# Part stores in one transfer a quarter, and three products of the first stage in other places

## The reference

```python
xn = _layernorm(x, axis=-1)
# _L0_attn_ref, on xn
x2 = _layer_norm(xn, ln1_g, ln1_b)
q, k, v = x2 @ wq + bq, x2 @ wk + bk, x2 @ wv + bv          # 16 heads of 16 channels
p = jnp.einsum('blhd,dm->blhm', x, proj_mat) / math.sqrt(D_HEAD)   # x: q or k, 128 maps
feature = jnp.concatenate([jnp.cos(p), jnp.sin(p)], axis=-1) / math.sqrt(D_KMAP)
kv = jnp.einsum('blhm,blhd->bhmd', kp, v)
attn = jnp.einsum('blhm,bhmd->blhd', qp, kv)
s = ...   # attn @ wo + bo, residual, layer norm, w1, relu, w2, residual
# _L0_ffn_ref, on xn
xr = mu_r * x + (1.0 - mu_r) * x_prev
xk = mu_k * x + (1.0 - mu_k) * x_prev
r = jax.nn.sigmoid(jnp.einsum('btc,dc->btd', xr, W_r))      # "receptance"
k_act = jnp.square(jax.nn.relu(jnp.einsum('btc,dc->btd', xk, W_k)))
out = r * jnp.einsum('btc,dc->btd', k_act, W_v)             # "value" product
x = x + s * _silu(out)
```

## Time and profile before

| what | us |
| --- | --- |
| median of 3 runs (range) | 2329.96 (2327.01 to 2332.29) |
| the profiled execution, device time | 2326.66 |
| its span, first to last instruction | 2324.9 |
| features of batch 0, first to last L456 | 57.33 to 157.07 |
| features of batch 1, first to last L456 | 280.57 to 379.06 |
| first L456 of batches 2 and 3 | 502.49, 722.41 |

### The profile page before, as it was taken

How to read it: one execution, slowest core, us unless ns; L and a number is a source line. 1 busy time by engine, 2 the same in 40 slices (tenths; PEclk the granted TensorE clock), 3 DMA queues, 4 the chain that set the end, 5 groups by cost and what they waited for, 6 DMA issues and landing times. The chain is left out here.

```text
span 2324.9 us, 24556 instructions
## 1 busy us (share of the span) xinstructions
PE 1963.6 (84%) x7316; PEld 1006.5 (43%) x7332; DVE 1717.9 (74%) x2363; ACT 1217.3 (52%) x1646; POOL 1223.2 (53%) x651
## 2 busy tenths in 40 slices
PE   5699879978996898889989998899886678997995
PEld 3336534643463355333324332433242235665663
DVE  4984598369827933699999999999989993223887
ACT  3873486268526732566654665466544433443542
POOL 2601351053107110288788899989977672212664
PEclk9899989989999999999999999999989999999997
DMA  6510640073007312788889898988899982223442
GB/s 163 137 37 0 163 108 20 0 200 83 9 19 182 73 37 64 107 300 290 284 278 313 283 284 291 317 282 294 288 307 373 329 302 76 93 89 100 136 136 79
DMA packets 182690, 402.57 MB, mean 173 GB/s; under 512 B 49454, under 2 KB 78384, under 8 KB 181410
## 3 DMA queue, kind: packets, MB, share of 16 engines
q1 hardware_dynamic: 170530, 371.10, 52.1%
q0 software_dynamic: 12032, 29.90, 4.5%
HBM read 356.30 MB, written 45.51 MB: 173 GB/s over the span
## 5 line engine op out<-in xcount | busy, mean ns | idle before, releaser
L1191 POOL TENSOR_TENSOR late<-late,rows 128x1024 f32<-128x1024 f32 x256 | 602.9, 2364 | 146.8 <-DVE late L1667 138.0
L1840 PE MATMUL m_Q<-late,ident_m 128*128 128x512 f32 x1024 | 528.9, 649 | 150.5 <-POOL late L1191 113.1
L1667 DVE TENSOR_TENSOR_SCAN late<-m_Q,late 128x1024 f32<-128x1024 f32 x256 | 586.2, 2290 | 44.8 <-ACT m_Q L1377 16.4
L1377 ACT ACTIVATE m_Q<-late,acol 128x1024 f32<-128x1024 f32 x256 | 286.1, 1118 | 361.5 <-DVE late L1667 359.3
L1840 PEld LDWEIGHTS m_Q<-late,ident_m 128*128 128x128 f32 x1024 | 195.4, 203 | 450.9 <-POOL late L1191 261.0
L1660 DVE TENSOR_TENSOR late<-m_Q,rows 128x1024 f32<-128x1024 f32 x256 | 306.9, 1199 | 12.8 <-DMA rows<-bc_s 12.7
L290 POOL TENSOR_TENSOR qkh<-early,qkh 128x1024 bf16<-128x1024 f32 x16 | 33.8, 2126 | 286.8 <-ACT qkh L561 286.8
L1559 ACT ACTIVATE late<-m_Q,e_b1c 128x128 f32<-128x128 f32 x312 | 88.9, 368 | 181.1 <-PE m_Q L1909 180.8
L456 DVE SCALAR_TENSOR_TENSOR early<-early,work 128x1024 f32<-128x1024 f32 x128 | 155.8, 1217 | 25.4 <-ACT early L598 23.0
L606 ACT ACTIVATE early<-early 128x1024 f32<-128x1024 f32 x128 | 134.8, 1053 | 49.1 <-DVE early L461 47.8
L1900 PE MATMUL m_Q<-early,late 128*128 x312 | 149.0, 600 | 2.7 <-issue 2.0
(11 more groups left out here) (233 smaller groups left out, 3393.5 us busy)
## 6 DMA issues: line engine op xcount, KB each, us to landing
rows<-bc_s SPq DMA_DIRECT2D x512, 512.0 KB, 5.8
rows<-st_s SPq DMA_DIRECT2D x64, 384.0 KB, 5.7
st_s<-qkh SPq DMA_DIRECT2D x128, 96.0 KB, 2.4
r_s<-late SPq DMA_DIRECT2D x39, 256.0 KB, 2.0
rows<-st_s SPq DMA_DIRECT2D x32, 256.0 KB, 6.5
xin<-in_x SPq DMA_DIRECT2D x4, 1024.0 KB, 10.2
xres<-in_x SPq DMA_DIRECT2D x4, 1024.0 KB, 7.3
mx_s<-s SPq DMA_DIRECT2D x4, 1024.0 KB, 4.5
```

The lines of the kernel that those rows point to most:

```text
L1191: nc.gpsimd.tensor_tensor(pr[:, n % NH, :], h[:, n % NH, :], cb[:, n % NCB, :], ALU.mult).then_inc(pr_ok, 1)
L1377: A(dA[:, :], dt[:, (b * KI + m) % 2, :], ACT.Exp, scale=acol[:, m, i % NS:i % NS + 1]).then_inc(dA_ok, 1)
L1667: v_.tensor_tensor_scan(h[:, n % NH, :], dA[:, :], dB[:, n % 2, :], 0.0, ALU.mult, ALU.add).then_inc(h_ok, 1)
L1840: ins = mm(half(Y, c), ident[:, :], half(pr[:, n % NH, :], c), start=False, stop=(n % NS == NS - 1), skip_group_check=True)
```

## The change

In `phase_a`, part stores: a quarter is stored by one transfer of 128 partitions instead of eight of 16, to a DRAM tensor with channels ahead of parts; a unit is loaded by four transfers (48, 48, 16, 16 partitions) instead of three (48, 48, 32). SP's order becomes store 0, unit 0, store 1, unit 1, store 2, and store 3 only inside the features, ahead of unit 2.

Products: `q1` leaves the stretch before the features and is made in steps 0 and 1; `xn`, `gl` and `gate` of the previous batch are made in steps 2, 4, 7 and 12. `kk` moves from steps 20 and 26 to 9 and 14, `vv` from behind `wo` to steps 20 and 25, and `r` from steps 13 and 17 to behind `wo`, with its Tanh reading PSUM. On POOL `low(3)` stands ahead of the mixtures, and xk is mixed before xr. In the scan, at nine steps a batch, ACT takes a link of a sigmoid before a PSUM evacuation instead of after it.

```diff
-AMID = {13: ("r", 0), 17: ("r", 1), 20: ("kk", 0), 26: ("kk", 1)}
-TAKEN = {15: ("r", 0), 19: ("r", 1), 22: ("kk", 0), 28: ("kk", 1)}
+AMID = {0: ("q", 1), 9: ("kk", 0), 14: ("kk", 1), 20: ("vv", 0), 25: ("vv", 1)}
+RELU = {11: 0, 16: 1}
+VALUE = {21: 0, 26: 1}
+PREVIOUS = {2: ("xn", 0), 4: ("xn", 1), 7: ("gl",), 12: ("gate",)}
...
 def parts_out(b, q):
     sp.wait_ge(lo_ok, b * 4 + q + 1)
-    for hd in range(8):
-        sp.dma_start(g["st_s"][q, hd].rearrange("s c t -> c s t"), parts[DH * hd:DH * hd + DH, q % 2, :, :]).then_inc(part_out[q % 2], 16)
+    sp.dma_start(g["st_s"][q].rearrange("h c s t -> (h c) s t"), parts[:, q % 2, :, :]).then_inc(part_out[q % 2], 16)
...
+def first_units(b):
+    parts_out(b, 0)
+    unit_in(b, 0)
+    parts_out(b, 1)
+    unit_in(b, 1)
+    parts_out(b, 2)
...
@@ SP @@
 def batch(b, last):
+    parts_out(b, 3)
+    unit_in(b, 2)
+    if b:
+        turned_out(b - 1)
+    unit_in(b, 3)
...
@@ POOL @@
 for b in range(B):
     pool.wait_ge(tr_ok, b * 6 + 4)
     if b:
-        pool.wait_ge(lg_ok, b)
+        pool.wait_ge(out_ok, b * 2)
+    low(b, 3)
+    pool.wait_ge(lo_ok, b * 4 + 4)
+    mixture(b, 1)
     mixture(b, 0)
-    mixture(b, 1)
...
@@ ACT, behind the two Sin of step s @@
+if s == 1:
+    high(b, 3)
+elif s == 3:
+    middle(b, 3)
+elif s in VALUE:
+    i = VALUE[s]
+    wait_full(ac, b, "vv", i)
+    A(kr[:, i, :], slot(b, "vv", i)[:, :], ACT.Identity).then_inc(vv_ok, 1)
...
@@ ACT, scan, step 15 of block1 @@
+sigmoid(b + 1, "conv", 1, 1)
 evacuate(b + 1, "z", 1, 0)
-sigmoid(b + 1, "conv", 1, 1)
```

More of the change, by code:

```diff
@@ L60, in sequence @@
     for b in range(B):
[L61 to L65, removed]
+        seq += body(b)
+        if b + 1 < B:
+            seq += [(b + 1, j) for j in PRE]
+        else:
+            seq += [(b, j) for j in [("mx", m) for m in range(2 * KD)] + [("xn", 0), ("xn", 1), ("gl",), ("gate",)]]
     return seq
@@ L213, in _ @@
                     load(t[:, :, :], matrix(n), a_in)
[L214 to L215 removed]
+                for s in range(3):
+                    for p in (0, 3 * DH):
+                        load(prj[p + s:p + 3 * DH:3, :], g["proj"], p_in)
+                for s in range(2):
+                    load(prj[(6 + s) * DH:(7 + s) * DH, :], g["proj"], p_in)
                 with nc.allow_non_contiguous_dma(reason="vectors by channel, once"):
@@ L509, in batch @@
                         remainder(b + 1, 2)
-                        remainder(b + 1, 3)
-                    wait_full(dv, b, "gate")
-                    v_.tensor_copy(g["lg"][:, bass.ds(b * TB, TB), :],
-                                   slot(b, "gate")[:, 0:TB * E].rearrange("p (t e) -> p t e", t=TB)).then_inc(lg_ok, 1)
+                    if last:
+                        gate_logits(b)
                     assert n[0] == (DVE_LINKS if last else DVE_LINKS + 2 * LN_LINKS)
@@ L524, in _ @@
                 prepare()
-                for q in range(4):
+                for q in range(3):
                     remainder(0, q)
@@ L542, in _, with high, middle @@
                 ac.wait_ge(prep, 4)
+                def high(b, q):
+                    name, m = SPLIT[q]
+                    wait_full(ac, b, name, m)
+                    if q >= 2 or b:
+                        ac.wait_ge(part_out[q % 2], (b * 2 + q // 2) * 16)
+                    A(parts[:, q % 2, 0, :], slot(b, name, m)[:, :], ACT.Identity, bias=cols[:, "qk".index(name), m:m + 1]).then_inc(hi_ok, 1)
+                def middle(b, q):
+                    ac.wait_ge(r1_ok, b * 4 + q + 1)
+                    A(parts[:, q % 2, 1, :], rest(q), ACT.Identity).then_inc(mid_ok, 1)
                 def before_features(b):
@@ L633, in batch @@
                             A(xi4[:, m, 3:3 + L], slot(b, "mx", m)[:, :], ACT.Identity).then_inc(mx_ok, 1)
-                        normed(b)
+                        for c in range(NC_):
+                            normed(b, c)
                         logits(b)
```

215 lines of the change are left out of this document (104 added, 111 removed).

## The result

| | before | after |
|---|---|---|
| median (range), 4 runs each | 2328.49 (2323.80 to 2332.29) | 2358.99 (2357.27 to 2360.53) |
| ratio, 95% interval | 1 | 1.0130 (1.0111 to 1.0149) |
| span of the profiled execution | 2324.9 | 2358.2 |

The changed kernel is 30.5 us slower. The prediction had the sign, 12 us of the amount, and a range that ended at 2354.

The account below looks back on a forecast made before the run. No engine was taken to bound the whole kernel; DVE sets the features' pace. 3 x 2.9 + 8.0 - 4.7 = +12.0 on 2326.66 gave 2338.7, as a median 2342, stated as 2341; range 2318 to 2354.

Parts of the forecast that it names:

- The start: Start of the features: first rounding subtraction 12.2 us earlier in batch 1, 5.6 earlier in batch 0.
- Steps 0 to 3: First feature steps: part of the gain given back, step 3 14.4 us behind the first subtraction where it was 9.1.
- Step 9: PE waits for the first mixture, late behind low(3), before kk; step 9 starts 5.5 us later in batch 1.
- Step 9 to the end (a small gain): Features from step 9 to the last subtraction: -2.6 us together, from copies, masks and evacuations.
- Batch 0: Features of the first batch: last subtraction 8 us later, with step 9 11 us later, less 2.6.
- The scan: Scan stage: a sigmoid link fills ACT's wait before an evacuation, DVE regains 4.7 us over three batch changes.
- More waits: Rival, slower still: late squares or kk and vv slots cost each batch 3 us more, 2353; chance 0.1.
- The mixture is in time: Rival, faster: the first mixture doesn't hold PE at step 9, 2293, or 2318 with half the wait; chance 0.25.
- It cancels: Rival, same: start, stall and scan come out within 4.7 us of nothing; chance 0.2.

Follow-up runs that it names:

- before_store: The kernel before with only the storage part of the change (one store a quarter, four loads a unit, their orders on SP and ACT): 2354.99 us, ratio 0.9993.
- before_scan: The kernel before with only the eight scan exchanges, sigmoid link ahead of the PSUM evacuation: 2355.67 us against 2358.36, ratio 0.9993.
- unit2_first: The changed kernel with SP loading unit 2 ahead of storing quarter 3: 2357.33 us, ratio 1.0121 to the kernel before.
- kk_later: The changed kernel with kk at steps 12 and 15, its relu at 14 and 17, vv at 22 and 26: 2375.74 us, ratio 1.0208.
- mix_first: The changed kernel with POOL's first mixture ahead of low(3) and unit 2 loaded ahead of store 3: 2348.07 us against 2358.50, ratio 0.9951.
- gate_read_13: The changed kernel with DVE's copy of the previous batch's gate logits in step 13, not 14: 2348.75 us, ratio 1.0086.
- mix_first_gate: mix_first with the edit of gate_read_13 added: ratio 0.9934 to the kernel before.
- q1_before_act_order: q1_before with gate logits read in step 13, gate product read behind step 6, and ACT's order ahead of the features changed: 2321.57 us, ratio 0.9859.
- q1_before: The changed kernel with the second query half and quarter 3 back ahead of the features: 2344.35 us, ratio 0.9946.

## Why the prediction was right in sign and short in size

Against the prediction's steps, in us. The whole was +12.0 predicted and +33.3 between the two spans.

- **The start.** Predicted -12.2; measured -12.6, -12.5 and -11.1 in batches 1 to 3: right. Batch 0: -5.6 predicted, -4.2 measured; there I gave it to the order of `middle` and to the second quarter's stores, and before_store, which has both, starts at 57.57, against 57.33 before and 59.62 in before_scan. So these two alone do not give it; what does stays open. This start also scatters: after, unit2_first and kk_later are alike up to there and start at 53.17, 53.59 and 50.30.
- **Steps 0 to 3.** Predicted 14.4 to step 3 and 20.0 to the end of `middle(3)`; measured 14.9 and 20.4. Right.
- **Step 9.** Predicted 43.6 behind the first subtraction, with the mixture at +40.0 and the half product at half clock, 3.7; measured 44.2 to 44.5, +40.0, 3.68. Right, and unit2_first shows that of unit 2 and the mixture the latter binds. What I did not see is the third wait at the same place (the gate product's slot, 2.49 us in mix_first), which costs nothing while the mixture is last. Before, step 9 stood at 25.2 and not 25.9 in batches 2 and 3, which makes the stall 0.7 longer there.
- **Step 9 to the end (a small gain).** This is the step that failed: its term of -2.6 counted copies, masks and evacuations and put PE's waits for PSUM slots at nothing. Predicted -2.6 a batch; measured +0.6, +2.1, +0.7, +1.0. That is 4.4 + 10.4 = 14.8 of the 21.3 us that the sum is short. gate_read_13 names about half of it: `kk(1)` in step 14 takes the slot of the gate logits, which DVE reads in step 14, and PE runs at half clock behind the wait. Without it these steps take 7.2 us less over the three batches that have a previous batch, and mix_first_gate takes 7.75 off mix_first there. Batch 0, which has no such wait, was 1.1 us shorter too, and 2.3 shorter in unit2_first (70.12), so part of its miss is scatter. With the wait gone, batches 0 to 3 are at -0.5, 0.0, -1.3 and -2.2 of before, and at -1.1 to -1.6 in batches 0 to 3 of mix_first_gate: the gain is there, but smaller than the -2.6, and why is not shown beyond what follows. The "about 1 us less by my count" for POOL beside DVE's masks did not come: the collision of the earlier trace rows moved to step 17, a mask of 4.09 us beside the bias that began 0.97 us earlier, as the timelines of DVE and POOL show:

```profile
355.70 4.09 DVE L488 TENSOR_SCALAR early<-early 128x1024 int32<-128x1024 int32 x1
```

```profile
354.73 4.51 POOL L314 TENSOR_TENSOR xn_a<-xn_a,bias 128x2048 f32<-128x2048 f32 x1
```

- **A count beside the sum.** DVE's work in the features was given as about 83 us; its own terms make 86, and the trace has 7.6 us of waits with a releaser and not 6. No term of the sum uses them.
- **Batch 0.** Predicted +8, measured +12.4: 3.2 from the step above, 1.4 from the start.
- **The scan.** Predicted -4.7. The two places of 1.80 us each gave 1.0. From the last subtraction of batch 3 to the end of the span it was 1504.9 us before and 1501.4 after, -3.5; not settled, as said above.
- **The rivals.** "More waits" came nearest, with the slots of `kk` and `vv` holding phases back, at 3 us a batch and chance 0.1; what the trace has is the reverse, `kk(1)` itself held by the slot of an older job. Batches 1 to 3 came out 4.6 to 6.2 us over the forecast of 2.9, and the slot of `kk(1)` alone made 2.0 to 3.2 of it. "The mixture is in time" had the right reason for what the stall costs: mix_first takes 35 us out of the first stage. Its 2293, 0.985 of 2328, was too low even so: mix_first came to 0.995, and to 0.9895 with the two slot waits gone, which it had left out. "It cancels" had nothing for it.

The chance of "more waits" was too low because I followed the rotation of PSUM slots only for the jobs that I knew to be in the features before. Three jobs of the previous batch came in among the phases (two transposes, the gate product, the gate logits), and each is read by another engine later than a phase would be. With three slots, whatever comes third behind such a job waits for that read.

## What to carry to other kernels

When a job is put into a rotation of a few buffers, write down for each job the one that held its buffer and when that is read: here `kk(1)` waited 4.43 us for the job three places ahead of it, which made the change dearer than forecast, and `kk(0)` had a second such wait hidden behind the mixture; both went with a read moved by one step. Where several waits end at one instruction, taking away the one that ends earlier gives nothing (unit2_first, 1.0121 against 1.0130), and taking away the last shows the next (mix_first, 2.49 us for the slot); so a gain worked out from the last one alone is an upper bound. And a stage that starts 12 us earlier gains only if what feeds its middle starts earlier too: with `low(3)` moved behind step 3, the mixture did not.

## What was not expected of the hardware

- The same kernel before ran at a median of 2328 us on one chip and 2358 us on two others, 1.3% apart, as much as the effect under study. The first stage agrees between them to some 2 us (the last subtraction of batch 3 at 820.01 in the first and 822.15 in before_scan); what is longer lies behind it: 1504.9 us from there to the end against 1539.3 there and 1536.0 in before_store. Why is not shown.
- A store of 768 KB in one transfer landed 4.5 us after its issue in the median, where 3.9 had been worked out by size; store 0 of batch 1, which that figure was for, was in after 3.3 (issued at 265.42, the load that waits for it at 268.70). The one of quarter 1 in q1_before_act_order, issued at 254.53 right behind the loads of unit 0, released ACT only at 262.3, 7.8 us later.
- A half product of four matmuls took 1.94 us at full clock, 3.60 to 3.78 behind waits of 1.9 to 9.8 us, and 2.81 us behind a wait of 2.46 and one of 0.33 us in gate_read_13. The length of the wait alone does not tell which: behind 2.49 us in mix_first it took 3.65, behind 3.12 us in q1_before 3.15, with a granted clock of 0.60 over it.
- A sign mask of DVE that began while POOL ran an operation with two inputs ended 0.55 us behind that operation's end, whatever its start: at 322.70 against 322.15 in the earlier trace rows, and in the changed kernel at 359.79 against 359.24, 338.61 against 338.05 and 320.88 against 320.33. So what such a mask costs is what is left of POOL's operation when it begins, and such masks took from 1.4 to 5 us.
